# Layers behind attention placed among the last two heads, by groups of 512 tokens, with outputs turned by transposing DMA

## What is computed

```python
q, k, v = x @ Wq, x @ Wk, x @ Wv                    # 16 heads of 64
attn = softmax(q @ k.T / 8 + causal)                # 2048 x 2048 for each head
x1 = norm(x + (attn @ v) @ Wo + bo)
x2 = norm(x1 + relu(x1 @ quant(W1).T + b1) @ quant(W2).T + b2)
x3 = norm(x2 + quantised_attention(x2))             # its output is pb where the bound holds
e = argmax(x3 @ Wg + bg); gate = max(softmax(x3 @ Wg + bg))
pos = position of the token among those of its expert  # a running count over tokens
y = gate * (relu(x3 @ W1[e] + b1[e]) @ W2[e] + b2[e]) if pos < 128 else 0
out = norm(x3 + y)
```

## Time and profile before

| Part of the profiled execution | from, us | to, us |
|---|---|---|
| attention, to the last weighing | 0 | 721.4 |
| layer0_rest | 721.4 | 851 |
| attention1_check (with the bound) | 851 | 868.8 |
| choosing, numbering, scattering, loading the rows | 871 | 904.2 |
| experts | 904.2 | 937 |
| sending back, last norm, output | 937 | 960.9 |
| **span of this execution** | | **960.9** |
| its own time | | 962.76 |
| median of the 3 timed runs | | 964.39 |

### The profile page before, as it was taken

One profiled execution on the slowest core, in us unless ns is written; L12 is line 12 of the kernel. 1 busy time (PEld: TensorE's weight loads), 2 busy tenths in 40 slices (PEclk: granted clock), 3 DMA queues, 4 the chain that ended last, 5 costly groups with the idle time before them and its releaser, 6 DMA issues. The chain is left out here.

```text
span 960.9 us, 25894 instructions
## 1 busy us (share of the span) xinstructions
PE 800.2 (83%) x10965; PEld 530.8 (55%) x10965; DVE 590.0 (61%) x1026; ACT 689.4 (72%) x953; POOL 624.5 (65%) x393
## 2 busy tenths in 40 slices
PE   5789999999999999999999999999986666542490
PEld 3345555666566666656666665666655554332390
DVE  5686777656666665666566665656776477375015
ACT  4357777888888878888888888788994766341263
POOL 6256768889888887888888888877004664113350
PEclk9799999999999999999999999999998997555695
DMA  6211133220230122023011301310006200040252
GB/s 169 46 35 35 29 78 74 57 45 2 51 84 2 35 44 59 2 51 83 4 36 24 78 2 42 72 23 2 2 2 211 68 1 2 0 89 24 77 183 89
DMA packets 58060, 48.31 MB, mean 50 GB/s; under 512 B 6602, under 2 KB 54344, under 8 KB 57814
## 3 DMA queue, kind: packets, MB, share of 16 engines
q1 hardware_dynamic: 56198, 43.60, 19.1%
q0 software_dynamic: 1024, 1.45, 0.5%
q10 hardware_dynamic: 720, 1.57, 0.5%
HBM read 16.64 MB, written 5.26 MB: 23 GB/s over the span
## 5 line engine op out<-in xcount | busy, mean ns | idle before, releaser
L670 POOL TENSOR_TENSOR prob_lo<-prob,prob_hi 128x896 f16<-128x896 f32 (+2 forms) x286 | 518.4, 1833 | 127.7 <-ACT prob L501 109.8
L559 DVE TENSOR_REDUCE part_max<-psum 128x2 f32<-128x1024 f32 (+1 forms) x320 | 334.2, 1060 | 110.9 <-PE psum L359 78.6
L498 ACT ACTIVATE prob_hi<-psum 128x1024 f16<-128x1024 f32 (+1 forms) x320 | 297.3, 930 | 119.2 <-PE psum L407 114.7
L501 ACT ACTIVATE prob<-psum 128x1024 f32<-128x1024 f32 (+1 forms) x320 | 296.9, 930 | 0.0
L404 PE MATMUL psum<-high 128*128 128x512 f16 (+3 forms) x640 | 224.5, 351 | 23.8 <-DVE part_max L559 8.3
L430 PE MATMUL psum<-v,prob_hi 128*128 128x65 f16 x2176 | 232.3, 193 | 3.9 <-DVE prob_lo L598 3.0
L434 PE MATMUL psum<-v,prob_lo 128*128 128x65 f16 x2176 | 230.4, 194 | 0.0
L432 PE MATMUL psum<-v,prob_hi 128*128 128x64 f16 x2176 | 230.4, 192 | 0.0
L430 PEld LDWEIGHTS psum<-v,prob_hi 128*128 128x128 f16 x2176 | 198.9, 98 | 45.3 <-issue 15.7
L407 PE MATMUL psum<-mixed 65*128 65x512 f16 (+3 forms) x640 | 220.6, 349 | 0.0
L432 PEld LDWEIGHTS psum<-v,prob_hi 128*128 128x128 f16 x2176 | 200.3, 97 | 13.3
(11 more groups left out here) (226 smaller groups left out, 1084.6 us busy)
## 6 DMA issues: line engine op xcount, KB each, us to landing
high<-kq SPq DMA_DIRECT2D x128, 128.0 KB
mixed<-kq SPq DMA_DIRECT2D x64, 128.0 KB
ew<-in_L_ffn_W SPq DMA_DIRECT2D x32, 256.0 KB
expert_rows<-heads_out SPq DMA_DIRECT2D x1, 1032.0 KB, 8.3
e_xe<-expert_rows SPq DMA_DIRECT2D x4, 258.0 KB, 3.7
prob<-in_L_attn_x SPq DMA_DIRECT2D x4, 256.0 KB, 6.7
mixed<-shift SPq DMA_DIRECT2D x64, 1.0 KB
eb<-in_L_ffn_b SPq DMA_DIRECT2D x1, 1024.0 KB
```

The costliest lines, as they stand in the source:

```text
L498: act.activation(m.prob_hi[i % HI_RING][:, 0:u.width], src, ACT.Exp, scale=EXP_SCALE)
L501: act.activation(m.prob[i % PROB_RING][:, 0:u.width], src, ACT.Exp, scale=EXP_SCALE)\
L559: last = dve.tensor_reduce(m.part_max[:, g % 2, :, r, c:c + 1], src[:, :, col:col + width], AX, ALU.max)
L670: pool.tensor_tensor(m.prob_lo[i % LOW_RING][:, c], m.prob[i % PROB_RING][:, c], m.prob_hi[i % HI_RING][:, c], ALU.subtract).then_inc(low_ ...
```

## The change

The heads' outputs are no longer kept in f32 and turned by PE. `normalise` writes them as two f16 halves, high and low, by one multiplication and four further instructions; when both heads of a pair have finished a group, SP turns the 128 x 1024 f16 block by a transposing DMA (`turn_out`). There are 32 of these, 28 of them for the first seven pairs.

Heads 14 and 15 change places group by group. Their jobs end before unit 290 (`REST`). From unit 292 on, the scores use two of the three buffers, and the two banks of the third take all intermediate results of the layers behind attention, one bank each (`FILLS`). A table (`tail_steps`) says beside which unit i each step runs, on each engine; group g of 512 tokens starts at unit `GROUP_AT[g]` = 294, 300, 309 and 324. The attention ends with unit 319, so group 3, and the last steps of group 2, come behind it. Each step stands in the engine's list behind the unit's own work. The low halves go to DVE for every third unit from 290 on, to POOL otherwise.

The standard deviation is found by two Newton steps on DVE (`one_over_deviation`, 11 small instructions) and no longer by ACT, in all four norms; moments come from bn_aggr. The third norm, the logits, choosing, numbering and scattering run by group too. `attention1_check` is gone as a block; its bound is worked out behind the numbering of group 3. The tables are filled during attention. The weights of the first eight experts and a 1 MB bias are loaded behind the last turning of outputs. Buffers lie at fixed places in one slab, where parts of attention that are done are used again.

```diff
 def all_units():
     order = [(head, g) for g in range(GROUPS) for head in range(2)]
-    order += [(head, g) for head in range(2, HEADS) for g in range(GROUPS)]
+    order += [(head, g) for head in range(2, HEADS - 2) for g in range(GROUPS)]
+    order += [(head, g) for g in range(GROUPS) for head in range(HEADS - 2, HEADS)]
...
+        some = BUFS if not isinstance(what, Unit) or what.index < REST + 2 else BUFS - 1
+        b = min(range(some), key=lambda b: (max(free[b], clock["pe"]), free[b]))
...
+GROUP_AT = (294, 300, 309, 324)
...
+    for g, i in enumerate(GROUP_AT):
+        for part in range(3):
+            put("pe", i - 2 + part, "project", g, part)
+        put("dve", i, "norm", g, 0)
+        put("dve", i + 1, "scale", g, 0)
+        put("pool", i + 2, "bias", g)
+        put("pe", i + 3, "turn", g, 0)
+        put("act", i + 3, "place", g, 0)
+        for f in range(UPS):
+            for engine in ("pe", "act", "pool"):
+                put(engine, i + 4 + f // 2, "up", g, f)
+        put("pe", i + 7, "down", g)
+        put("dve", i + 7, "norm", g, 1)
+        put("dve", i + 8, "scale", g, 1)
+        put("dve", i + 9, "third", g)
+        put("pe", i + 10, "turn", g, 1)
+        put("act", i + 10, "place", g, 1)
+        put("pe", i + 11, "turn3", g)
+        put("act", i + 11, "place3", g)
+        put("pe", i + 12, "gate", g)
+        put("dve", i + 12, "choose", g)
...
+        put("pe", i + 14, "count", g)
+        put("dve", i + 14, "slots", g)
+        for k in range(4):
+            put("pool", i + 15 + k, "scatter", g, k)
...
+def one_over_deviation(dve, c, out, variance, work):
+    v, half, s, q = work
+    c.mark(dve.tensor_scalar(v, variance, EPS, None, ALU.add))
+    c.step(dve.tensor_scalar(half, variance, EPS, 0.5, ALU.add, ALU.mult))
+    c.step(dve.tensor_scalar(s.bitcast(I32), v.bitcast(I32), 1, None, ALU.logical_shift_right))
+    c.step(dve.tensor_scalar(s.bitcast(I32), s.bitcast(I32), ROOT_BITS, None, ALU.add))
+    for _ in range(2):
+        c.step(dve.reciprocal(q, s))
+        c.step(dve.tensor_tensor(q, q, half, ALU.mult))
+        c.step(dve.scalar_tensor_tensor(s, s, 0.5, q, ALU.mult, ALU.add))
+    c.step(dve.reciprocal(out, s))
...
             def normalise(u):
-                out = m.heads_out[:, 4 * u.group:4 * u.group + 4, u.head * HD:(u.head + 1) * HD]
...
+                dve.tensor_tensor(hi, acc[:, :, 0:HD], inv.unsqueeze(2).broadcast_to([P, 4, HD]), ALU.mult)\
+                    .then_inc(out_high, 1)
+                dve.wait_ge(out_high, u.turn + 1)
+                for r in range(4):
+                    last = dve.scalar_tensor_tensor(lo[:, r, :], acc[:, r, 0:HD], inv[:, r:r + 1], hi[:, r, :], ALU.mult,
+                                                    ALU.subtract)
...
+            def turn_out(u):
+                pair, g = u.head // 2, u.group
+                sp.wait_ge(acc_free, u.turn + 1)
+                sp.wait_ge(t.turned_in[g], 16 * pair)
+                sp.dma_start_transpose(m.turned[:, g, pair, :].rearrange("p (a n) -> p a n", n=P), m.rows(pair, g))\
+                    .then_inc(t.turned_in[g], 16)
...
             for i in range(NU):
                 exponents(UNITS[i])
...
+                tail(i)
+            for i in range(NU, STEPS):
+                tail(i)
```

## The result

The changed kernel takes **978.86 us** (median of 4 runs, 972.89 to 979.11), the kernel before 965.03 in the same comparison: a ratio of 1.013 (1.008 to 1.017). It is slower; the forecast was 940 with a range of 902 to 970.

| Stretch | before | forecast | after | miss |
|---|---|---|---|---|
| attention, to unit 290's exponential | 672.4 | 675.4 | 684.2 | 8.8 |
| unit 290 to the last weighing | 49.0 | 132 | 154.2 | 22.2 |
| last weighing to the first expert product | 184.7 | 70.9 | 78.7 | 7.8 |
| from there to the end | 54.8 | 59.0 | 59.8 | 0.8 |
| span | 960.9 | 936.3 | 976.9 | 40.6 |

What follows compares the result with a forecast made beforehand. Attention's end was taken as bound by ACT with PE close behind, what follows by latency. 960.9 less 109.6 behind the last weighing, plus 82 in the last units and 3 in attention, gave 936.3, forecast as 940; range 902 to 970.

Steps and rivals of the forecast that it cites:

- the mechanism: Attention: `normalise` takes about 0.65 us more, 56 times, mostly while DVE would wait for PE; cost 3 us, 0 to 10.
- the walk through the units: Units 290 to the last weighing, added up piece by piece, each ending at an exponential: 132 us against 50, 82 lost.
- holds: Last 30 units: DVE instructions lengthened until a POOL instruction ends; 14 us for some 14 encounters.
- 1.6 us of waiting for each copy: Last 30 units, ACT: a turned copy waits for scores 0.9, turning 0.45, latency 0.25; the unit takes 4.3 instead of 1.8.
- 150 what comes out if nothing overlaps: Upper end of the 100 to 150 us kept for the last 30 units; ACT's sum of 90 was the floor.
- the block's end: Behind attention: scatters 5.1, SP's wake 1.2 and four loads 5.05, together 11.4 us, then two block boundaries 2.3.
- Rival 2: POOL's port, last 30 units: POOL holds DVE instructions for its whole length, 63 us instead of 14; time 977; chance 0.10.
- Rival 1: Last 30 units: the pieces overlap, DVE's backlog under ACT's slow units, near 100 us; time 908; chance 0.24.
- Rival 3: Slow transposes in attention: from 15 us each the maxima come late, from 19 the gain is gone; chance 0.06.
- Rival 4: Behind attention: group 3's chain waits for weights or PE's clock, 15 to 25 us more, 960 or so; chance 0.10.
- The signs given ahead: What the trace after should show, from attention's pace to the experts' end, including 71 us behind attention and 59 from there.
- the signs of being wrong: Stretch at ACT's 90 with DVE waiting, PE waiting for sends in attention, or the chain behind attention over 85 us.

Runs made afterwards that it cites:

- e6: Changed kernel with the heads' outputs' low halves replaced by zeros, so the projection reads rounded outputs; span 966.4 us, unit 290 starting at 673.54.
- e4: Changed kernel with all low halves of the probabilities from unit 290 on made by DVE, none by POOL; span 970.4 us.
- e7: Changed kernel with only group 0 beside attention and groups 1 to 3 behind it; span 974.2 us.
- e8: Changed kernel, but only group 0's steps up to its second norm beside attention, at wide distances, with DVE's low halves moved; everything else behind; span 948.1 us.
- e5: Changed kernel with matmuls that nobody reads put ahead of PE's known stops beside the last units; span 979.9 us.
- e10: e9 with the experts' rows waited for by TensorE in the experts' block and the last norms overlapped; median 931.83 us, ratio 0.966 to the kernel before.
- e1: Changed kernel with all four groups behind attention and three score buffers kept to the end; median 961.07 us, ratio 0.997 to the kernel before.
- e9: e1 with the square root of every norm made by ACT again instead of Newton steps on DVE; span 937.1 us.

## Why the prediction was wrong

**Attention before unit 290: the leak was mis-sized.** The forecast had the mechanism, 37 us more on DVE, and let 3 of them through, 0 to 10 at most. DVE's busy time grew from 435.6 to 480.4 (37 counted, and the early steps at units 283 to 288), and 12 came through. e6 shows that the division has 10.7 of them. I took DVE's idle time as cover, but row maxima stand behind the division in DVE's list, and PE waits for their buffers: these waits grew by 8.6 us and fell back by 8.0 in e6. Of the division's 37 us more than a quarter came through, not a twelfth.

**The last 30 units: the step that failed** is the walk through the units. It made DVE the bound, over 80% busy, with PE waiting for its low halves, and PE "not the bound". DVE's sum was met within a tenth: 95 and 14 of holds forecast, 100 measured, 18 of it in instructions longer than the shortest of their form. But DVE is 65% busy, PE waits for none of its low halves, and e4 gave it 11 us more without any change of the stretch. What the runs show instead is that the lists alternate: a turning 3 units behind a norm comes up 5 us before its input, and then scores, exponentials, low halves and weighing all wait in order behind it; when it is through, DVE waits for them. I had written the two halves of this down, 1.6 us of waiting for each copy and "150 what comes out if nothing overlaps", and took 132. The measured 154.2 lies just over the end that I had called the upper bound. Laid beside the trace, the walk falls behind all along: from unit 290's exponential to that of units 294, 300, 306 and 313 and to the last weighing it has 11.8, 36.6, 68.3, 104.2 and 132 us; the trace has 15.6, 44.4, 78.9, 119.0 and 154.2. The evidence for the stops is in the waits above and in e7 and e8: up to its second norm the same group costs 30 us beside attention with narrow distances and 17 with wide ones, where it saves 28 behind.

PE's work was mis-sized too: 77 us forecast, all but at full clock (the forecast's own parts, 43 and three times 12, make 79), 107 measured at 0.76. Against the forecast this is more than the whole miss: PE's time without work is 47 us, and the forecast had left 55. The clock is at 0.98 in e8, where the stops are gone, so its fall goes with the stops; but how much of the stretch's length comes from matmuls at half clock, and how much from the stops themselves, isn't separated by any run. That the real matmuls got 26 us shorter in e5 says how large the clock's part could be.

**Behind attention: right but for three terms.** The chain to the end of group 3's projection took 15.5 us (15 forecast), turning to the end of the net 12.6 (12.4), second norm 6.5 (6.6), third 5.3 (5.4). The first norm took 8.0 instead of 6.6, one copy held by POOL among it; turning, logits, choosing and numbering 8.5 instead of 7.4. The largest miss is the block's end, 18.6 us from the last slots to TensorE instead of 13.7: SP issues the loads from 902.11 to 904.14, each lands 4.2 us (the median of the four) after its issue, the last at 908.2, and only then do two block boundaries begin. They take 5.4 us, while I had 2.3 for both; the other 1.8 us missed lie in scatters and loads. e10 took 3.3 us of it away.

```profile
902.11 2.03 SPq L1597 DMA_DIRECT2D xe<-expert_rows  x4
```

```profile
913.68 1.73 PE L1922 MATMUL psum<-ident,xe 128*128 128x128 f32 x7 [18.79 <-PEq L1639]
```

The end was forecast as 59.0 and measured 59.8.

**The rivals.** Rival 2, POOL's port, named 977, and the span is 976.9; it was still wrong. It wanted 63 us of holds in DVE's instructions, and 18 us are all that these are longer than their shortest. The right number is luck: it came from another cause. Holds exist, and look as in the earlier trace rows: a shift of 128 x 4 elements takes 1.74 us beside a low half of POOL, and 0.17 elsewhere:

```profile
705.97 1.74 DVE L526 TENSOR_SCALAR root<-root 128x4 int32<-128x4 int32 x1
...
745.35 0.17 DVE L526 TENSOR_SCALAR root<-root 128x4 int32<-128x4 int32 x1
```

```profile
703.70 3.99 POOL L1444 TENSOR_TENSOR prob_lo<-prob,prob_hi 128x1024 f16<-128x1024 f32 x2 [8.20 <-ACT prob L1023]
```

Rival 1 (overlap, 908) wanted the 30 units near 100 us, and they took 154. Rival 3 is excluded: the transposes land in 3.1 us (the median; the slowest of all takes 10.3, under the 15 that it wanted of each), near what the forecast took from a load of the same size.

```profile
turned<-turned SPq DMA_TRANSPOSE x28, 3.1
```

The Trainium skill gives two prices here. Advanced Engine Details and Errata, X-Bar Transpose (TRN2), as fast as ordinary DMAs: this trace agrees, 3.1 us beside 4.2 for a plain load of 258 KB. VectorE: DVE Perf Modes, The three transpose paths, 1309 ns for one 128 x 128 block: for eight of them a plain multiple gives an estimate of 10.5 us, which this trace doesn't bear out.

Rival 4 (a longer chain, 960) held in part: 7.8 us, not 15 to 25, and no wait of PE in it is for weights.

**The signs given ahead.** "Attention's pace to unit 290 within 10 us of 660" was a slip: unit 290 starts at 672.4 in the kernel before. Seen as foretold: ACT waiting for scores, small DVE instructions lengthened, transposes under 5 us, a clock near half behind attention with no engine over half busy. Not seen: DVE over 80% busy, PE waiting for DVE's low halves, 132 us. None of the signs of being wrong came either (a stretch of 90 us with DVE waiting, PE waiting for sends, a chain of over 85 us): they had no case in which the stretch is longer than its sum.

**The largest error** is none of the terms. The forecast compared the change with the kernel before and asked how much of the overlap is lost. e1 is the comparison that was missing: the new tail by itself, pipelined over four groups and behind attention, needs 161.5 us where the old one needed 184.7, and 53.1 ahead of it. Against that the placement had to save more behind attention than it cost beside it. The forecast's own numbers, 82 us more beside and 109.6 less behind, mixed both gains, so that the rebuilding's share, 23 us behind attention, was credited to the placement.

## What to carry to other kernels

Work put into another loop's in-order lists paid here when each step stood further behind its input than the input takes (e8), and cost time when it didn't (e7). A step that comes up early stops everything behind it on its own engine and then, in turn, the engine that it waited for. Before placing work, measure the same work unplaced: it separates what the new form gives from what the place gives. Where the sums of all engines stay well under the length of a stretch, ask first which waits it is made of. Beside attention DVE could take 11 us more (e4) without a change of the stretch; behind attention, where DVE was about as full, 1.44 us less in each of twelve norms gave 17.4 (e9), since each norm stood in the chain.

## What the runs showed of the hardware

- Switching ACT between exponential and square root costs one table load of 1.28 us, and it lay in idle time in e9, ahead of the first root:

```profile
745.06 1.28 ACT L1080 ACT_TABLE_LOAD   x1
748.89 0.21 ACT L1080 ACTIVATE root<-root 128x4 f32<-128x4 f32 x1 [2.54 <-DVE root L554]
```

The Trainium skill, ScalarE: Activation LUTs, Table sets: the hidden batching unit, gives about 2.7 us for one load and 5.3 us for the two of an exponential and a square root; the one load in these rows takes 1.28 us, half of its figure.

- Four bn_aggr of 128 x 6 take 0.38 us together; the five small steps for the same moments in the kernel before take 0.76 us, from 841.94 to 842.70 (the first of them in the earlier trace rows):

```profile
705.24 0.38 DVE L541 BATCH_NORM_AGGREGATE mv<-stats 128x2 f32<-128x6 f32 x4
```

- Two block boundaries cost more than the 2.3 us that I had for them: the last load lands at 908.2, and TensorE starts at 913.68, 5.4 us later.
